# A running sum of router masks moves from GpSimd to the vector engine, and positions are worked out in float

## The chip, the cores and the metric

The kernel runs on one core of a Trainium2 chip, as one launch. A core has five engines with an instruction stream each: the tensor engine (PE, matmuls and transposes), the vector engine (DVE), the scalar engine (ACT), GpSimd (POOL) and SyncE (SP), which here issues most DMAs. Each engine runs its instructions in the order in which they were written; between engines, and between two instructions of one engine where one reads what the other wrote, the program waits on semaphores. The metric is device time in microseconds of one execution, lower is better.

## The reference, cut to what matters

Two layers of gated cross-attention with a feed-forward block run on 4 x 1024 tokens of 256 features. The first layer's feed-forward block is a mixture of 64 experts, 8 per token, with at most 128 tokens for each expert. What the change touches is the place of each token in its expert's list:

```python
w, idx = jax.lax.top_k(probs, TOP_K)
e_flat = idx.reshape(-1)
tok = jnp.arange(A) // TOP_K
onehot = jax.nn.one_hot(e_flat, E, dtype=jnp.int32)
pos = jnp.take_along_axis(jnp.cumsum(onehot, axis=0) - 1, e_flat[:, None], axis=1)[:, 0]
slot = jnp.minimum(pos, CAPACITY)
buf = jnp.zeros((E, CAPACITY + 1, H), x.dtype).at[e_flat, slot].set(x[tok])
```

The position of a token is the number of earlier tokens that picked the same expert.

## The kernel before

The kernel has three stages: the first layer's attention with the router, the experts (with the shared expert and the preparation of the second layer's weights beside them), and the second layer. Only the first stage, up to some 345 us, holds lines that the change touches.

The first stage goes over eight halves of 512 tokens (`h` from 0 to 7; each batch of 1024 tokens has two). A half has four tiles of 128 tokens. Its main work is the attention over 154 keys for 16 heads: PE computes scores (L838 to L841) into five banks of PSUM, ACT makes two passes over them (`square` L1200, `root` L1205), DVE one (`weight`, L1557, 0.68 us a time), and PE multiplies the weights with the values (L862, L867). Beside it run, each in small steps, the keys of the next batch (`key_mask`, L1512 and L1514, before every second half), the queries of the next half (PE L827, DVE `q_high` L1545 and `q_low` L1551 into `q_stage`), the end of the attention of the half before (transposes L884, `divide` L1563 and L1565, output projection L908 and L913, `x_add` L1578), and the router.

The router of a half: `gate` gives 64 logits per token; DVE takes the eight highest (`top`, L1604), marks them (`pick`: L1611 and then L1616, which writes `masks`, four tiles of 128x64, ones and zeros); PE's `count` multiplies the masks with a triangular matrix and with ones, and adds the product of ones with `mask_sums` (called `before` in the code), the number of picks per expert and lane in all halves before this one. `mask_sums` has two places that take turns; for the next half the new one is the old one plus the four tiles of masks. In the kernel before, POOL makes these four adds (`count` of the GpSimd program, L2009). DVE's `position` (L1636) takes the product of `count` out of PSUM, subtracts 4096 where a token picked the expert, and writes integers; `ranks` (L1641, L1643, L1646, L1647) splits them into the part over 16 and the rest, both as bf16 in `pos_a` and `pos_b`, which lie in the tile `w_con_fused`. From these, `hots` (L1745, L1748) makes one-hot tiles later, from which PE builds the lists of tokens (L1026).

The order is fixed when the program is built. A planner lays the units of all streams into slots, with tables that say in which slot of the attention each step of a half goes; every engine then runs the units that it has a part in, in the order of the one plan. `pick`, `count`, `position` and `ranks` stand in it one after another for each half, with attention units, and in places keys and queries, between them. PE's part of `count` and DVE's `position` share a bank of PSUM with the queries, keys and projections (two banks, `misc`, in turn).

Of the kernel before, what the change touches and what calls it, by code (L numbers as in the profile page):

```python
# [14 lines left out]
ALU = mybir.AluOpType  # L15
# [14 lines left out]
HT = HALF // P  # L30
HALVES = TOKENS // HALF
# [27 lines left out]
NB = 16  # L59
# [3 lines left out]
FAR = 4096.0  # L63
# [434 lines left out]
def build(nc, D, out):  # L498
    ctx = ExitStack()
    with ctx:  # L500
# [13 lines left out]
        misc = Ring(bank[6:8], sems("misc_full", 2), sems("misc_free", 2))  # L514
# [19 lines left out]
        rstd = [sb(f"rstd{i}", [P, HT], F32) for i in range(2)]  # L534
# [17 lines left out]
        with ExitStack() as scope:  # L552
# [35 lines left out]
            masks = s0("masks", [P, HT, EXPERTS], BF16)  # L588
# [187 lines left out]
        def tensor_program(T):  # L776
# [155 lines left out]
            def count(h):  # L932
                key = ("count", h)
                if h == 0:
                    T.wait_ge(upper_in, 16)
                    T.wait_ge(pool_set, POOL_FIRST)
                else:
                    T.wait_ge(summed, HT * h)
                T.wait_ge(masked, h + 1)
                T.wait_ge(*misc.vacant(key))  # L940
                for t in range(HT):
                    here = misc.ap(key)[:, t * EXPERTS:(t + 1) * EXPERTS]
                    T.matmul(here, upper[:, :], masks[:, t, :], start=True, stop=False)
                    for u in range(t):
                        T.matmul(here, ones[:, :], masks[:, u, :], start=False, stop=False)
                    m = T.matmul(here, ones[:, :], before[:, h % 2, :], start=False, stop=True)
                m.then_inc(misc.fills(key), 1)
# [467 lines left out]
        def vector_program(V):  # L1415
            own = Own()
# [190 lines left out]
            def pick(h):  # L1607
                first = gated_tiles(h).start
                V.wait_ge(dve_own, own.n)
                for t in range(HT):  # L1610
                    m = V.match_replace(picked[:, t, :], top[:, first + t, :], probs[:, first + t, :], 1.0)  # L1611
                m.then_inc(dve_own, own.up())
                if h:
                    V.wait_ge(summed, HT * h)
                V.wait_ge(dve_own, own.n)
                V.tensor_scalar(masks[:, :, :], picked[:, :, :], 0.0, None, ALU.is_gt).then_inc(masked, 1)  # L1616

            def gate_weights(b):
# [10 lines left out]
                                       gate_sums[:, 0, :].unsqueeze(2).to_broadcast([P, GATED_TILES, EXPERTS]),  # L1629
                                       ALU.mult, ALU.mult).then_inc(rows_set, 1)  # L1630

            def position(h):
                key = ("count", h)
                counts = misc.ap(key)[:, 0:HT * EXPERTS].rearrange("p (t n) -> p t n", n=EXPERTS)
                V.wait_ge(*misc.filled(key))
                V.scalar_tensor_tensor(pos_i[:, 0, :, :], masks[:, :, :], -FAR, counts, ALU.mult,  # L1636
                                       ALU.add).then_inc(misc.frees(key), 1)

            def ranks(h):
                V.wait_ge(*misc.freed(("count", h)))  # L1640
                V.tensor_scalar(pos_i[:, 1, :, :], pos_i[:, 0, :, :], 4, None,  # L1641
                                ALU.arith_shift_right).then_inc(dve_own, own.up())
                V.tensor_scalar(pos_i[:, 0, :, :], pos_i[:, 0, :, :], NB - 1, None,  # L1643
                                ALU.bitwise_and).then_inc(dve_own, own.up())
                V.wait_ge(dve_own, own.n)
                V.tensor_scalar(pos_a[:, HT * h:HT * h + HT, :], pos_i[:, 1, :, :], FAR / NB, None, ALU.add)  # L1646
                V.tensor_copy(pos_b[:, HT * h:HT * h + HT, :], pos_i[:, 0, :, :])  # L1647


# [225 lines left out]
            def out_add(h, b, k):  # L1875
                if k == BURST - 1:
# [4 lines left out]
                    for two in range(HT // 2):  # L1881
# [7 lines left out]
            units = {"bn": bn, "highest": highest_, "ranks": ranks, "q_high": q_high, "q_low": q_low, "stats": stats_, "norm": norm, "key_mask": key_mask, "bias_parts": set_bias_parts, "key_rest": key_rest,  # L1889
                     "set_values": set_values, "weight": weight,  # L1890
                     "divide": divide, "x_add": x_add, "shift": shift, "top": top_, "pick": pick,
                     "gate_weights": gate_weights, "position": position, "sh_split": sh_split_, "sh_up": sh_up,
                     "sh_inner": sh_inner_, "sh_down": sh_down, "taps": set_coef, "matrix": stage_matrix, "across": across,
                     "hid_bias": set_hid_bias, "out_bias": set_out_bias, "hots": hots, "lists": set_lists,
                     "tokens": set_tokens, "gate_up": gate_up, "down": down, "add_experts": add_experts,
# [12 lines left out]
        def gpsimd_program(G):  # L1908
# [86 lines left out]
                    G.tensor_tensor(w_sd[:, 1], sd_staged, w_sd[:, 0].bitcast(F32),  # L1995
                                    ALU.subtract).then_inc(sh_split, 1)

            def count(h):
                if h == HALVES - 1:
                    return  # L2000
                old, new = before[:, h % 2, :], before[:, (h + 1) % 2, :]
                G.wait_ge(masked, h + 1)
                if h:
                    G.wait_ge(*misc.filled(("count", h - 1)))
                    G.wait_ge(summed, HT * h)
                for t in range(HT):
                    if t:
                        G.wait_ge(summed, HT * h + t)
                    G.tensor_tensor(new, new if t else old, masks[:, t, :], ALU.add).then_inc(summed, 1)  # L2009

            def set_query_ones(i):
                G.wait_ge(pool_set, set_.n)
                G.memset(q_stack[i][STACK:ROWS0, :, :].bitcast(F32), 1.0).then_inc(pool_set, set_.up())
# [8 lines left out]
            def clear_rest():  # L2022
# [14 lines left out]
            G.memset(k_masked[:, :, 2, :], 0.0).then_inc(pool_set, set_.up())  # L2037
            set_query_ones(0)
            G.wait_ge(pool_set, set_.n)
            units = {"count": count, "sh_weights": sh_weights, "sh_split": sh_split_, "rstd": norm_rstd, "load_rest": clear_rest, "gather": gather, "down": scatter,  # L2040
                     "add_experts": add_experts, "bias_out": bias_out, "up": hidden_rest, "clear_v1": clear_v1}
            for n, plan in enumerate((first, experts, last)):
                if n == 2:
# [350 lines left out]
```

## Time and profile before

| What | Value |
| --- | --- |
| Median of 3 runs | 1139.92 us (1139.42 to 1140.05) |
| The profiled execution | 1139.42 us |
| Its span, first to last instruction | 1137.6 us |
| Mean granted clock of PE | 0.957 of full speed |
| Busy: PE, DVE, ACT, POOL | 989.6, 777.7, 622.1, 402.9 us |
| Chain that ended last, by engine | PE 54%, DVE 22%, ACT 9%, POOL 4%, DMA 3% |
| First stage, 0 to 344 us: PE, DVE, ACT, POOL busy | 292.9, 281.0, 245.9, 56.9 us |

Instructions of one engine overlap a little at their ends, so the start of one can lie before the end of the one ahead. The chain of waits is followed back from the last instruction to what released it, or to the instruction ahead of it on its engine; a piece in it is the time from one such step to the next. A window's row gives the busy time of each engine, with the number of instructions in brackets.

### The profile page before, as it was taken

What the parts mean: (1) busy time and instruction counts of PE and PEld (TensorE: products, weight loads), DVE (VectorE), ACT (ScalarE), POOL (GpSimd) and SP (SyncE); (2) the same over time, 40 slices, a digit from 0 to 9 for tenths busy, and PEclk for the clock granted to TensorE, in tenths of its full rate; (3) what the DMA queues carried; (4) which work ended last, traced back from release to release, by engine and by line L of the source; (5) the groups of instructions that cost most, each with busy time, mean ns of one, the idle gap of its engine ahead of it and who ended that gap; (6) DMA issues with size and microseconds to landing.
All of it is one profiled execution on the core that took longest, in us unless ns stands there. A gap on an engine that the chain in (4) does not pass through costs nothing.

```text
span 1137.6 us, 16837 instructions
## 1 busy us (share of the span) xinstructions
PE 989.6 (87%) x5379; PEld 702.5 (62%) x5379; DVE 777.7 (68%) x1951; ACT 622.1 (55%) x1204; POOL 402.9 (35%) x417
## 2 busy tenths in 40 slices
PE   4899999999769699998999758788898989989988
PEld 2355555555447488776887636466667666757657
DVE  4688989987787566657675666866775676664443
ACT  1887888879465245546554213654554555454532
POOL 6000111102020257677776222152525252504234
PEclk9899999999979899999999958899999999999999
DMA  6737466453114378888876533413231412110000
GB/s 139 205 73 214 141 175 171 109 151 112 56 52 152 107 175 192 195 231 209 211 178 133 131 85 100 100 35 113 58 94 28 113 51 86 29 49 1 21 19 19
DMA packets 101559, 128.38 MB, mean 113 GB/s; under 512 B 31136, under 2 KB 73504, under 8 KB 101216
## 3 DMA queue, kind: packets, MB, share of 16 engines
q1 hardware_dynamic: 87088, 106.32, 32.8%
q0 software_dynamic: 12288, 18.88, 9.3%
q10 hardware_dynamic: 2096, 2.10, 0.8%
q8 instruction: 44, 0.72, 0.3%
q14 instruction: 43, 0.35, 0.1%
HBM read 66.15 MB, written 30.70 MB: 85 GB/s over the span
## 4 chain that ended last, share of the span: by engine, by line
PE 54%; DVE 22%; ACT 9%; issue 5%; POOL 4%; DMA 3%; SPq 1%; ACTq 1%; DVEq 0%; POOLq 0%
PE psum L960 6%; PE psum L1144 6%; PE psum L1129 5%; PE psum L1049 4%; PE psum L976 4%; PE psum L867 3%; PE psum L838 3%; DVE peaks L1825 3%; DVE stats L1421 2%; PE psum L913 2%; PE psum L784 2%; PE psum L827 2%; PE psum L1076 2%; PE psum L862 2%; DVE weights L1557 2%
## 5 line engine op out<-in xcount | busy, mean ns | idle before, releaser
L1924 POOL TENSOR_SCALAR vareps<-moments 128x4 f32<-128x4 f32 x32 | 12.2, 382 | 350.0 <-DVE moments L1431 350.0
L838 PE MATMUL psum<-q_stack,k_stack 97*128 97x512 f32 (+1 forms) x256 | 118.3, 488 | 20.2 <-DVE weights L1557 7.2
L1355 ACT ACTIVATE weights<-psum 128x512 f32<-128x512 f32 x160 | 92.9, 595 | 65.6 <-PE psum L838 57.5
L1947 POOL DMA_INDIRECT expert_sums<-made,sum_rows x64 | 104.1, 1626 | 63.6 <-DVE made L1789 44.4
L1076 PE MATMUL psum<-k_stack,q_stack 96*128 96x308 f32 x256 | 86.3, 399 | 36.5 <-DVE peaks L1825 24.6
L1557 DVE SCALAR_TENSOR_TENSOR weights<-weights,psum 128x512 f32<-128x512 f32 x160 | 102.7, 681 | 17.8 <-ACT weights L1205 17.5
L1825 DVE TENSOR_REDUCE peaks<-psum 128x2 f32<-128x308 f32 x256 | 105.8, 470 | 7.7 <-PE psum L1076 7.5
L1979 POOL TENSOR_TENSOR hidden<-hidden_whole,hidden 128x512 fp32r<-128x512 f32 x64 | 82.9, 1300 | 60.7 <-DVE hidden L1873 60.7
L960 PE MATMUL psum<-feat_parts,w_shared_up 128*128 128x512 f32 x384 | 98.4, 406 | 4.2 <-DVE shared_silu L1663 2.6
L1076 PEld LDWEIGHTS psum<-k_stack,q_stack 96*128 96x128 f32 x256 | 50.8, 203 | 81.7 <-DVE peaks L1825 40.1
L1144 PE MATMUL psum<-w_con_high,hidden 128*128 128x256 f32 x512 | 100.7, 295 | 0.5 <-POOL hidden L1979 0.5
L1200 ACT ACTIVATE weights<-psum 128x512 f32<-128x512 f32 x160 | 89.1, 596 | 20.7 <-PE psum L838 20.0
L1873 DVE CAST hidden<-hidden_whole 128x512 fp32r<-128x512 f32 x64 | 45.9, 725 | 77.5 <-ACT hidden_whole L1384 77.0
L1939 POOL DMA_INDIRECT got<-rows_scratch,tokens x64 | 68.3, 1068 | 76.5 <-issue 73.7
L1205 ACT ACTIVATE weights<-weights 128x512 f32<-128x512 f32 x160 | 94.0, 633 | 1.0
L1129 PE MATMUL psum<-feats,w_up_high 128*128 128x512 f32 x256 | 80.4, 411 | 11.3 <-ACT hidden_whole L1384 6.4
L1144 PEld LDWEIGHTS psum<-w_con_high,hidden 128*128 128x128 f32 x512 | 81.2, 190 | 13.3 <-POOL hidden L1979 7.6
L960 PEld LDWEIGHTS psum<-feat_parts,w_shared_up 128*128 128x128 f32 x384 | 71.4, 193 | 19.9 <-DVE shared_silu L1663 3.3
L838 PEld LDWEIGHTS psum<-q_stack,k_stack 97*128 97x128 f32 (+1 forms) x256 | 48.0, 192 | 56.2 <-issue 19.8
L1384 ACT ACTIVATE hidden_whole<-psum,hidden_bias 128x512 f32<-128x512 f32 x64 | 42.6, 687 | 66.2 <-PE psum L1129 48.0
L1049 PEld LDWEIGHTS psum<-got_t,expert_w 128*128 128x128 f32 x512 | 64.3, 191 | 23.0 <-ACT got_t L1311 14.5
L1049 PE MATMUL psum<-got_t,expert_w 128*128 128x128 f32 x512 | 70.3, 280 | 8.9 <-DVE inner L1782 4.1
(210 smaller groups left out, 2219.9 us busy)
## 6 DMA issues: line engine op xcount, KB each, us to landing
expert_w<-in_expert_w SPq DMA_DIRECT2D x64, 384.0 KB
q_stack<-q_stage SPq DMA_DIRECT2D x96, 128.0 KB, 2.4
q_stack<-q_stage SPq DMA_DIRECT2D x174, 64.0 KB, 2.0
expert_sums<-zeros SPq DMA_DIRECT2D x6, 1408.0 KB, 8.6
fetched<-expert_sums SPq DMA_DIRECT2D x14, 512.0 KB, 4.5
k_raw<-in_k SPq DMA_DIRECT2D x16, 300.0 KB
x<-in_x SPq DMA_DIRECT2D x8, 512.0 KB, 4.8
rows_scratch<-rows SPq DMA_DIRECT2D x8, 512.0 KB, 3.5
```

The lines of the kernel that those rows point to most:

```text
L838: T.matmul(to, keys_of(h, head), q[0:row, head // 2, :], start=True, stop=True).then_inc(scored, 1)
L960: m = T.matmul(shared_banks(h).ap(key, half), w_sgu[:, pw, a:a + P], sh_parts[:, pf, c * HALF:(c + 1) * HALF], start=n == 0 and c == 0, st ...
L1049: m = T.matmul(bank[2][:, part * P:(part + 1) * P], expert_w[e % 8][:, c, part * INNER:(part + 1) * INNER], got_t[e % 3][:, c, :], start=c ...
L1076: T.matmul(wide.ap(key, i)[:, 0:2 * KEYS], q[0:STACK, p, t * P:(t + 1) * P], keys[0:STACK, 2 * KEYS * p:2 * KEYS * (p + 1)], start=True, s ...
L1129: m = T.matmul(wide.ap(key), up_parts[pw][:, c, k * P:(k + 1) * P], feats[:, pf, c, :], start=i == 0 and c == 0, stop=i == 2 and c == CD - 1)
L1144: m = T.matmul(out_bank[t // 2][:, t % 2 * DIM:(t % 2 + 1) * DIM], hidden[k][:, ph, t * P:(t + 1) * P], con_parts[pw][:, BURST * b + k, :] ...
L1200: A.activation(weights[n % 9][:, :], score_bank[n % 5], ACT.Square, bias=2.0, scale=-1.0).then_inc(squared, 1)
L1205: A.activation(weights[n % 9][:, :], weights[n % 9][:, :], ACT.Abs_reciprocal_sqrt).then_inc(exped, 1)
L1355: A.activation(weights1[n % 6][:, :], score_bank[n % 2], ACT.Exp).then_inc(exped, 1)
L1557: V.scalar_tensor_tensor(weights[n % 9][:, :], weights[n % 9][:, :], 1.0, score_bank[n % 5], ALU.min, ALU.max).then_inc(weighted, 1)
L1825: V.tensor_reduce(peaks[:, t, 2 * p:2 * p + 2], view, AX.X, ALU.max).then_inc(wide.frees(key, i), 1)
L1947: G.indirect_dma_start(sum_dram[e % SUMS], bass.IndirectOffsetOnAxis(ap=sum_rows[:, e:e + 1], axis=0), made[e % 4][:, :], None, bounds_che ...
```

## The change

The four adds of `count` move from POOL to DVE. There each add waits for the one ahead, and the semaphore `summed` rises once for a half, no longer once for an add; what waits for it waits for `h` instead of `4 * h`. The wait in `pick` for `summed` is dropped. `position` is three instructions now: the product goes to the float tile `picked`, 4096 is added there, and a copy casts to integers, which are now the positions themselves where a token picked the expert, and values from 4096 up where it didn't. In `ranks` the shift becomes a logical one, a wait is put between it and the mask of the low bits, and a plain copy takes the place of an add of 256.

```diff
@@ PE, count
-                    T.wait_ge(summed, HT * h)
+                    T.wait_ge(summed, h)
@@ DVE, pick
-                if h:
-                    V.wait_ge(summed, HT * h)
                 V.wait_ge(dve_own, own.n)
@@ DVE
+            def count(h):
+                if h == HALVES - 1:
+                    return
+                old, new = before[:, h % 2, :], before[:, (h + 1) % 2, :]
+                V.wait_ge(masked, h + 1)
+                for t in range(HT):
+                    if t:
+                        V.wait_ge(dve_own, own.n)
+                    elif h:
+                        V.wait_ge(summed, h)
+                    m = V.tensor_tensor(new, new if t else old, masks[:, t, :], ALU.add)
+                    if t < HT - 1:
+                        m.then_inc(dve_own, own.up())
+                m.then_inc(summed, 1)
+
             def position(h):
...
-                V.scalar_tensor_tensor(pos_i[:, 0, :, :], masks[:, :, :], -FAR, counts, ALU.mult,
+                V.scalar_tensor_tensor(picked[:, :, :], masks[:, :, :], -FAR, counts, ALU.mult,
                                        ALU.add).then_inc(misc.frees(key), 1)
+                V.wait_ge(*misc.freed(key))
+                V.tensor_scalar(picked[:, :, :], picked[:, :, :], FAR, None, ALU.add).then_inc(dve_own, own.up())
+                V.wait_ge(dve_own, own.n)
+                V.tensor_copy(pos_i[:, 0, :, :], picked[:, :, :]).then_inc(dve_own, own.up())
 
             def ranks(h):
-                V.wait_ge(*misc.freed(("count", h)))
+                V.wait_ge(dve_own, own.n)
                 V.tensor_scalar(pos_i[:, 1, :, :], pos_i[:, 0, :, :], 4, None,
-                                ALU.arith_shift_right).then_inc(dve_own, own.up())
+                                ALU.logical_shift_right).then_inc(dve_own, own.up())
+                V.wait_ge(dve_own, own.n)
                 V.tensor_scalar(pos_i[:, 0, :, :], pos_i[:, 0, :, :], NB - 1, None,
                                 ALU.bitwise_and).then_inc(dve_own, own.up())
                 V.wait_ge(dve_own, own.n)
-                V.tensor_scalar(pos_a[:, HT * h:HT * h + HT, :], pos_i[:, 1, :, :], FAR / NB, None, ALU.add)
+                V.tensor_copy(pos_a[:, HT * h:HT * h + HT, :], pos_i[:, 1, :, :])
@@ POOL
-            def count(h):
...
-                for t in range(HT):
-                    if t:
-                        G.wait_ge(summed, HT * h + t)
-                    G.tensor_tensor(new, new if t else old, masks[:, t, :], ALU.add).then_inc(summed, 1)
```

The first place is DVE's row in halves 1 and 3, from the masks to the first query step and the position, before the change (`k_masked` is the key masking, `weights` the attention's weights):

```order
L1616 TENSOR_SCALAR masks<-picked 128x256
L1512 TENSOR_SCALAR k_masked<-psum,bk,side_of 128x128 x2
L1514 SCALAR_TENSOR_TENSOR k_masked<-psum,bk,place_of 128x4x26
L1512 TENSOR_SCALAR k_masked<-psum,bk,side_of 128x128 x2
L1514 SCALAR_TENSOR_TENSOR k_masked<-psum,bk,place_of 128x4x26
L1545 TENSOR_SCALAR q_stage<-psum,bq 128x512
L1551 SCALAR_TENSOR_TENSOR q_stage<-psum,bq,q_stage 128x512
L1557 SCALAR_TENSOR_TENSOR weights<-weights,psum 128x512 x2
L1636 SCALAR_TENSOR_TENSOR pos_i<-masks,psum 128x256
```

And the same place after it:

```order
L1514 SCALAR_TENSOR_TENSOR k_masked<-psum,bk,place_of 128x4x26
L1640 TENSOR_TENSOR mask_sums<-mask_sums,masks 128x64 x4
L1545 TENSOR_SCALAR q_stage<-psum,bq 128x512
L1551 SCALAR_TENSOR_TENSOR q_stage<-psum,bq,q_stage 128x512
L1557 SCALAR_TENSOR_TENSOR weights<-weights,psum 128x512 x2
L1649 SCALAR_TENSOR_TENSOR picked<-masks,psum 128x256
L1652 TENSOR_SCALAR picked<-picked 128x256
L1654 CAST pos_i<-picked 128x256
```

The four adds stand between the key masking and the query step, and two more instructions behind the product. In halves 0, 2 and 4 there is no key masking, and the adds follow the masks at once. The second place is DVE in half 6, where the attention is nearly over; `sums` and `att` are the division of a tile's attention. Before:

```order
L1616 TENSOR_SCALAR masks<-picked 128x256
L1636 SCALAR_TENSOR_TENSOR pos_i<-masks,psum 128x256
L1563 RECIPROCAL sums<-psum 128x16
L1565 TENSOR_TENSOR att<-psum,sums 128x256
L1641 TENSOR_SCALAR pos_i<-pos_i 128x256
L1643 TENSOR_SCALAR pos_i<-pos_i 128x256
```

After:

```order
L1614 TENSOR_SCALAR masks<-picked 128x256
L1640 TENSOR_TENSOR mask_sums<-mask_sums,masks 128x64 x4
L1649 SCALAR_TENSOR_TENSOR picked<-masks,psum 128x256
L1652 TENSOR_SCALAR picked<-picked 128x256
L1654 CAST pos_i<-picked 128x256
L1563 RECIPROCAL sums<-psum 128x16
L1565 TENSOR_TENSOR att<-psum,sums 128x256
L1658 TENSOR_SCALAR pos_i<-pos_i 128x256
L1661 TENSOR_SCALAR pos_i<-pos_i 128x256
```

Six instructions more stand between the masks and the division here. In half 7 no adds are made, since no half follows. The rows of PE and ACT are the same before and after; POOL loses its 28 adds and keeps the order of the rest.

## Rows read from the trace of the kernel before

**Rows 1.** Windows view: PE, PEld, DVE, ACT, POOL busy (instructions); clock, DMA share, GB/s.
```profile
80.00:240.00 160.00, 150.92 (x790) 85.74 (x786) 145.92 (x409) 129.75 (x244) 20.64 (x40) 1.00 0.59 162
```

**Rows 2.** Waits, 60 to 340 us: us in total, times, longest us.
```profile
POOL mask_sums L2009 <- DVE masks L1616: 53.4, 7, 10.9
PEld psum L943 <- POOL mask_sums L2009: 0.9, 2, 0.5
```

**Rows 3.** Line 2009: duration ns min/median/max, first and last start, form.
```profile
L2009 POOL TENSOR_TENSOR mask_sums<-mask_sums,masks x28: 304/306/309, 96.9 to 295.0; 128x64 bf16<-128x64 bf16 x28
```

**Rows 4.** Groups on DVE, 60 to 340 us: busy us, mean ns, idle before.
```profile
L1748 DVE TENSOR_TENSOR hot_b<-b_iota,w_con_fused 128x1024 bf16<-128x1024 bf16 x21 | 14.4, 685 | 0.0
L1745 DVE TENSOR_TENSOR hot_a<-a_iota,w_con_fused 128x512 bf16<-128x512 bf16 x22 | 9.2, 420 | 2.2 <-PE psum L1026 2.2
L1474 DVE TENSOR_SCALAR normed<-x,moments,rstd 128x256 f32<-128x256 f32 x20 | 6.9, 413 | 0.0
L1588 DVE COPY sgate<-psum 128x4 f32<-128x4 f32 x8 | 1.2, 154 | 0.0
```

**Rows 5.** Timeline of DVE, ranks of half 7: start us, us, instruction.
```profile
335.24 0.29 DVE L1641 TENSOR_SCALAR pos_i<-pos_i 128x256 int32<-128x256 int32 x1
335.44 0.29 DVE L1643 TENSOR_SCALAR pos_i<-pos_i 128x256 int32<-128x256 int32 x1
335.77 0.29 DVE L1646 TENSOR_SCALAR w_con_fused<-pos_i 128x256 bf16<-128x256 int32 x1
```

**Rows 6.** Timeline of DVE, halves 0, 2 and 4: start us, us, instruction, idle before.
```profile
97.76 0.75 DVE L1545 TENSOR_SCALAR q_stage<-psum,bq 128x512 fp32r<-128x512 f32 x1 [0.94 <-PE psum L827]
...
101.37 0.75 DVE L1545 TENSOR_SCALAR q_stage<-psum,bq 128x512 fp32r<-128x512 f32 x1 [0.56 <-PE psum L827]
...
113.20 0.75 DVE L1578 SCALAR_TENSOR_TENSOR x<-psum,tanh_gates,x 128x512 f32<-128x512 f32 x1 [0.33 <-PE psum L913]
...
165.20 0.75 DVE L1545 TENSOR_SCALAR q_stage<-psum,bq 128x512 fp32r<-128x512 f32 x1 [0.86 <-PE psum L827]
...
234.38 0.75 DVE L1545 TENSOR_SCALAR q_stage<-psum,bq 128x512 fp32r<-128x512 f32 x1 [0.79 <-PE psum L827]
```

**Rows 7.** Chain of waits, half 1: start us, us, piece.
```profile
130.89 0.10 DVE k_masked L1514
131.04 0.76 DVE q_stage L1545
132.63 2.00 PE psum L827 x4
```

**Rows 8.** Chain of waits, ranks of half 3.
```profile
212.00 0.20 DVE pos_i L1641
```

**Rows 9.** Timeline of DVE, half 5.
```profile
265.40 0.29 DVE L1616 TENSOR_SCALAR masks<-picked 128x256 bf16<-128x256 f32 x1
...
265.61 1.28 DVE L1557 SCALAR_TENSOR_TENSOR weights<-weights,psum 128x512 f32<-128x512 f32 x2
...
267.74 0.25 DVE L1563 RECIPROCAL sums<-psum 128x16 f32<-128x16 f32 x1
...
269.20 0.26 DVE L1563 RECIPROCAL sums<-psum 128x16 f32<-128x16 f32 x1 [0.76 <-PE psum L884]
```

**Rows 10.** Timeline of DVE, half 6.
```profile
293.52 0.29 DVE L1616 TENSOR_SCALAR masks<-picked 128x256 bf16<-128x256 f32 x1
294.52 0.42 DVE L1636 SCALAR_TENSOR_TENSOR pos_i<-masks,psum 128x256 int32<-128x256 bf16 x1 [0.71 <-PE psum L946]
295.06 0.26 DVE L1563 RECIPROCAL sums<-psum 128x16 f32<-128x16 f32 x1
```

**Rows 11.** Chain of waits, position of half 7.
```profile
334.06 0.33 DVE pos_i L1636
```

**Rows 12.** Timeline of DVE, rows of half 7.
```profile
315.33 5.00 DVE L1474 TENSOR_SCALAR rows<-x,moments,rstd 128x256 f32<-128x256 f32 x3 [1.64 <-POOL rstd L1929]
```

**Rows 13.** Timeline of POOL beside it.
```profile
315.17 2.34 POOL L1992 TENSOR_TENSOR feat_parts<-feats_m,feat_parts 128x1024 fp32r<-128x1024 f32 x1
```

More of the change, by code:

```diff
@@ L1891, in vector_program @@
                      "divide": divide, "x_add": x_add, "shift": shift, "top": top_, "pick": pick,
-                     "gate_weights": gate_weights, "position": position, "sh_split": sh_split_, "sh_up": sh_up,
+                     "gate_weights": gate_weights, "count": count, "position": position, "sh_split": sh_split_, "sh_up": sh_up,
                      "sh_inner": sh_inner_, "sh_down": sh_down, "taps": set_coef, "matrix": stage_matrix, "across": across,
@@ L1996, in sh_split_ @@
                                     ALU.subtract).then_inc(sh_split, 1)
-            def count(h):
[L1999 to L2005, printed above, removed]
-                for t in range(HT):
-                    if t:
-                        G.wait_ge(summed, HT * h + t)
-                    G.tensor_tensor(new, new if t else old, masks[:, t, :], ALU.add).then_inc(summed, 1)
             def set_query_ones(i):
@@ L2039, in gpsimd_program @@
             G.wait_ge(pool_set, set_.n)
-            units = {"count": count, "sh_weights": sh_weights, "sh_split": sh_split_, "rstd": norm_rstd, "load_rest": clear_rest, "gather": gather, "down": scatter,
+            units = {"sh_weights": sh_weights, "sh_split": sh_split_, "rstd": norm_rstd, "load_rest": clear_rest, "gather": gather, "down": scatter,
                      "add_experts": add_experts, "bias_out": bias_out, "up": hidden_rest, "clear_v1": clear_v1}
```

## The prediction

> **What bounds the kernel now.** I read the busy time by windows first, then the chain of waits, then the waits of the moved work, then the timeline of the vector engine (DVE) around each of the eight halves (0 to 7) of 512 tokens. The change touches only the first stage. There the tensor engine (PE) is busy 150.9 of 160 us and DVE 145.9, at a granted clock of 1.00, while GpSimd (POOL) is busy 20.6 [rows 1]. PE and DVE take turns: the reader is to see in the chain that DVE pieces stand on it wherever PE waits for a result (a DVE `q_stage`, then PE's query projection, [rows 7]), and that DVE has only short gaps of its own. So a DVE instruction costs its full time where no gap follows, and nothing where one does. The working goes by place, not by the sum of busy time.
>
> **What is removed.** POOL loses 28 adds of 0.306 us, 8.6 us [rows 3]. POOL sat 53.4 us waiting for the masks before them; the only wait charged to them is 0.9 us in 2 cases, on PE's load for the count [rows 2]. That product reads the running sum of the half before, finished a half earlier, so the charge is to a releaser long done. I take the removal at 0, with 0.9 us as the most it could give. The wait on `summed` in `pick` goes too; it was for the half before, so nothing is late in its place. PE's count still waits for the masks alone in effect.
>
> **Unit prices on DVE.** The profile shows two spacings of a 256-column instruction of 0.29 us. Without a wait in between the next starts 0.20 after (335.24 to 335.44); where it waits for the one ahead, 0.33 after (335.44 to 335.77) [rows 5]. So a waited instruction costs its duration + 0.04, an unwaited one its duration - 0.09.
> - Add 128x64 bf16: not shown. 1024 columns take 0.685 and 512 take 0.420 [rows 4]; the line through both gives 0.265 per 512 and 0.155 fixed, so 64 columns take 0.155 + 0.033 = 0.19. Bounds: 0.154, the smallest copy [rows 4], and 0.306, POOL's own time [rows 3]. I take 0.19, since its two rows are the same kind of operation and type.
> - Scale-and-add and cast of 128x256 f32 in SBUF: not shown in these types. The nearest are the 0.29 us ones on int32 [rows 5]; bounds 0.154 and 0.413, a 128x256 f32 operation with two scalars per partition [rows 4]. I take 0.29, by the like form.
> - The product of masks and counts keeps its 0.42 us [rows 10]; only its output goes to a float tile.
>
> So `count` is four adds, each waiting for the one ahead: in a dense run 3 x 0.23 + 0.10 = 0.79 us; right behind the masks it waits for them too, 0.04 + 3 x 0.23 + 0.10 = 0.83 after their end. `position` becomes three instructions: product 0.42 + 0.04, scale-and-add 0.33, cast 0.20 = 0.99 to the next one, where 0.33 was needed [rows 11]: +0.66 in a dense run, or 0.57 after the product's end. `ranks` gets one more wait between its first two: 0.33 - 0.20 = +0.13.
>
> The trace shows 0.13 us between the waited and the unwaited start [rows 5]. The Trainium skill (VectorE: DVE Perf Modes, section The DRAIN you can't avoid) says the opposite, that a semaphore between operations of DVE costs nothing extra, since the next has to wait for the pipeline to empty anyway. By that rule the added waits would be free; this trace disagrees, and the case stands below as a rival worked from the unwaited spacing.
>
> **The sum, half by half.**
> - Halves 0, 2, 4: `count` lands in the gap ahead of `q_stage`, where DVE waited 0.94, 0.86 and 0.79 us for PE's projection [rows 6]. It needs 0.83: 0, 0 and +0.04.
> - `position` in halves 0 to 4 lands in a gap too, 0.56 us ahead of the second `q_stage` of half 0 [rows 6], with four more of the same kind. It needs 0.57: +0.01 each, 0.05.
> - Half 1: between the masks and `q_stage` stands the key masking. The chain runs from its last piece at 130.89 into `q_stage` at 131.04, then PE's projection at 132.63 [rows 7]; no gap. `count` goes in exactly there: +0.79. Behind `q_stage` are queued its low part, PE's second projection and all the weights that follow.
> - Half 3: the same layout, +0.79; and here the chain passes through `ranks` too (212.00, [rows 8]): +0.13. In halves 0, 1, 2 and 4 a gap for PE's output projection follows `ranks` (0.33 at 113.20, [rows 6]) and takes the 0.13. Together 0.92.
> - Half 5: no keys, no queries; weights follow the masks at once (265.40, 265.61). `count` moves them by 0.83 + 0.29 - 0.21 = 0.91, `position` adds 0.66: 1.57. The gap ahead of the reciprocal at 269.20 was 0.76 [rows 9]: DVE was free at 268.44, now at 270.01, and the reciprocal starts 0.09 before that, 269.92. PE's weighing moves by less. +0.72.
> - Half 6: masks 293.52, the adds fill the 0.71 gap and overrun it: product at 293.52 + 0.29 + 0.83 = 294.64 rather than 294.52, reciprocal at 294.64 + 0.99 = 295.63 rather than 295.06 [rows 10], +0.57; `ranks` right behind, +0.13. 0.70.
> - Half 7: no count. The chain is DVE alone there, the product with 0.33 [rows 11] and then one-hots: 0.66 + 0.13 = 0.79.
>
> Sum: 0.04 + 0.05 + 0.79 + 0.92 + 0.72 + 0.70 + 0.79 = 4.0 us. What follows (the tail of the stage, the experts, the second layer) has no work changed and starts that much later. The profiled execution took 1139.42 us (its span 1137.6 and 1.8 around it), so 1143.4; against the median of the three runs, 1139.92, which lies 0.5 above it, 1143.9 us.
>
> Both ends: adds at 0.154 take 0.04 off each of four in halves 1, 3, 5 and 6 and the 0.04 of half 4, -0.7; the two new f32 operations at 0.154 take another 0.27 per half in 5, 6 and 7, -0.8: +2.5. Adds at 0.306 add 0.46 per half in 1, 3, 4, 5, 6 and 0.35 and 0.43 in 0 and 2, +3.1; the f32 operations at 0.413 add 0.24 in all eight, +1.9: +9.0.
>
> **Rivals.**
> 1. Waits inside DVE cost nothing. Adds are then 0.10 apart, `count` 0.40, `position` +0.40, `ranks` 0. Halves 1 and 3 give 0.40 each, 7 gives 0.40, 6 gives 0.19 (its product stays at 294.52, the reciprocal goes to 295.25), 5 next to nothing: +1.4, 1141.3 us. Against it stand the 0.20 and 0.33 of [rows 5]. 5%. The rule of the Trainium skill quoted above would have it so.
> 2. The new instructions are long, near the upper bounds, by a slower mode of the f32 ones or a longer small add: +6 to +9, about 1147 us. For it: the 0.413 row has the same shape and type [rows 4]. Against: 0.29 for all three forms of [rows 5]. 12%.
> 3. The clock falls once more, because PE idles a little longer. It stood at 1.00 in the attention [rows 1]; one projection of 2.00 us [rows 7] at the lower level (1.2 instead of 2.4 GHz) would take 4.00: +2 on top, 1145.9 us. 8%.
> 4. Not slower: the stage's tail gives it back. At 315.33 three `rows` instructions of DVE take 5.00 us [rows 12] where such a shape takes 0.413 each [rows 4], beside POOL's split from 315.17 [rows 13]. If `rows` got clear of the split, some 3.7 us would come back: +0.3, 1140.2 us. It decides on whether the split starts 1.1 us or more later against `rows` than it does (three instructions of 0.413 being done by then). Against: both stand behind POOL's `rstd`, and both move with DVE's one-hots. 5%.
> 5. Halves 1 and 3 don't bind: another path through PE, with slack of a microsecond, takes their 0.79 and 0.92, and the 0.9 of [rows 2] was real: +1.4, 1141.3 us. Against: the chain runs through both places without a gap [rows 7, 8]. 5%. Only rivals 4 and 5 together, 1137.6, or something unseen, would come out faster.
>
> **How the numbers follow.** The forecast has 65%, between 1142.4 and 1146; the rivals 5, 12, 8, 5 and 5. About 0.2% (2.3 us) is what a measurement of this kernel can tell from no change, so same is 1137.6 to 1142.2. Rivals 1, 4 and 5 lie there, 15%, less the 3% that I give to faster: same 0.12; faster by more than that 0.03; slower 0.85. The range goes from just above rivals 1 and 5, at 1141.5, up through rival 3 and the nearer part of rival 2 to 1147.3.
>
> **What would show it.** The four adds on DVE at 0.19 each, 0.23 apart; the two f32 instructions at 0.29; DVE's busy time in the first stage up by some 10 us (28 x 0.19 + 16 x 0.29) and POOL's down by 8.6. `q_stage` of halves 0, 2 and 4 still waiting for PE with next to no gap, that of halves 1 and 3 late by 0.8 and PE's projection behind it too. Against a same-numbered event of before the lag should be 0.8 after half 1, 1.8 after half 3, 2.6 after half 5, 3.3 after half 6, and 4.0 when the experts start, and stay. I would be wrong if PE's projection in half 1 is not late, if the adds start 0.10 apart, or if the lag shrinks in the tail at the `rows` instructions.

## The result, and the profile after

The changed kernel is slower: 1145.4 us in the median of 6 runs (1144.32 to 1147.23) against 1139.31 (1136.51 to 1140.05) for the kernel before, measured beside it, a ratio of 1.0059 with a 95% interval of 1.0046 to 1.0072. Measured a second time, with the last experiments, it was 1.0049 (1.0034 to 1.0065). The forecast was 1143.9 us, +4.0, where +6.1 came; the time lies inside the range of 1141.5 to 1147.3. The profiled execution took 1145.61 us, its span is 1143.8 us, 6.2 more than before.

The windows view of the changed kernel, 80 to 240 us, with the columns of [rows 1]:

```profile
80.00:240.00 160.00, 148.59 (x776) 84.83 (x773) 150.19 (x436) 127.75 (x240) 14.47 (x20) 1.00 0.59 162
```

DVE is busy for 150.2 of 160 us now, 4.3 more, and POOL for 14.5, 6.2 less; PE does less in the same stretch of time, since its work runs later. Over the whole span DVE's busy time went from 777.7 to 788.8 us.

The new instructions, by line (duration in ns: least, median, most; first and last start; form):

```profile
L1640 DVE TENSOR_TENSOR mask_sums<-mask_sums,masks x28: 181/192/193, 96.7 to 297.3; 128x64 bf16<-128x64 bf16 x28
```

```profile
L1652 DVE TENSOR_SCALAR picked<-picked x8: 293/294/295, 101.0 to 337.7; 128x256 f32<-128x256 f32 x8
```

```profile
L1654 DVE CAST pos_i<-picked x8: 293/294/295, 101.3 to 338.0; 128x256 int32<-128x256 f32 x8
```

So the adds take 0.192 us where 0.19 was estimated, and the two float instructions 0.294 where 0.29 was.

To see where the time went, take the same event in both traces and subtract the starts: the lag is how much later the event comes in the changed kernel. The two executions differ by 0.18 us before the first changed instruction; that is taken off. Lag in us, worked out from the timelines of DVE:

| Event | Lag | Forecast by then |
| --- | --- | --- |
| `q_stage` of half 0, behind the adds | 0.35 | 0 |
| `q_stage` of half 1 | 1.26 | 0.8 |
| `q_stage` of half 3 | 2.15 | 1.6 |
| `x_add` of half 3, behind `ranks` | 2.29 | 1.75 |
| `q_stage` of half 4 | 2.36 | 1.8 |
| reciprocal of half 5 (269.20 before) | 3.05 | 2.6 |
| one-hot behind `ranks` of half 6 | 3.65 | 3.3 |
| one-hot behind `ranks` of half 7 | 4.23 | 4.0 |
| last shared-expert step ahead of the lists | 4.40 | 4.0 |
| expert 7's `inner`, some 50 us on | 6.05 | 4.0 |

The last row holds the part that the forecast had not: 1.7 us appear behind the lists, where no instruction was changed.

The timeline of DVE after, in halves 0, 1 and 4 (start us, us, instruction; the idle time before it and what ended it in brackets), beside [rows 6, 7]:

```profile
96.67 0.87 DVE L1640 TENSOR_TENSOR mask_sums<-mask_sums,masks 128x64 bf16<-128x64 bf16 x4
97.93 0.75 DVE L1545 TENSOR_SCALAR q_stage<-psum,bq 128x512 fp32r<-128x512 f32 x1 [0.38 <-issue]
...
131.24 0.86 DVE L1640 TENSOR_TENSOR mask_sums<-mask_sums,masks 128x64 bf16<-128x64 bf16 x4
132.12 0.75 DVE L1545 TENSOR_SCALAR q_stage<-psum,bq 128x512 fp32r<-128x512 f32 x1
...
235.67 0.87 DVE L1640 TENSOR_TENSOR mask_sums<-mask_sums,masks 128x64 bf16<-128x64 bf16 x4
236.56 0.75 DVE L1545 TENSOR_SCALAR q_stage<-psum,bq 128x512 fp32r<-128x512 f32 x1
```

In half 4 the adds fill the gap that DVE had and overrun it by little. In half 1 `q_stage` starts 0.88 after the first add (0.79 was forecast). In half 0 the adds end at 97.54, PE's projection at 97.44, and still `q_stage` starts only at 97.93. The reader is to see that "issue" stands where PE stood in [rows 6]: DVE waits for nothing that the profile shows.

The clock's part. Windows view behind the lists, before:

```profile
375.00:380.00 5.00, 3.74 (x17) 3.77 (x18) 1.01 (x6) 0.00 (x0) 2.31 (x2) 0.50 0.95 339
380.00:385.00 5.00, 3.92 (x15) 2.88 (x13) 3.26 (x18) 1.18 (x3) 4.00 (x4) 0.81 0.57 186
385.00:390.00 5.00, 3.06 (x11) 1.51 (x11) 4.67 (x15) 3.14 (x8) 0.00 (x0) 1.00 0.13 38
```

And after, 4 us later, the same work:

```profile
379.00:384.00 5.00, 3.55 (x17) 3.48 (x17) 1.16 (x6) 0.00 (x0) 2.27 (x2) 0.50 0.95 328
384.00:389.00 5.00, 5.00 (x16) 3.93 (x15) 2.31 (x16) 1.17 (x3) 3.78 (x5) 0.55 0.60 197
389.00:394.00 5.00, 2.78 (x8) 1.47 (x7) 4.33 (x13) 1.62 (x5) 0.25 (x1) 0.79 0.16 51
```

The column behind POOL's is the granted clock of PE: 0.50 is the lower level, 1.2 GHz, 1.00 the upper, 2.4 GHz. PE had stood idle for the lists in both. Afterwards before's second window is at 0.81 and the third back at 1.00; after's are at 0.55 and 0.79. The chain shows the price on one group of matmuls, before and after:

```profile
380.44 3.49 PE psum L960 x12
```

```profile
384.73 4.56 PE psum L960 x12
```

The same twelve matmuls of the shared expert took 1.07 us longer. The next group of matmuls on the chain, before and after:

```profile
387.88 0.71 PE psum L1008 x2
```

```profile
392.20 2.28 PE psum L1008 x4
```

By the lag of the instructions of DVE around them, the first group took the lag from 4.48 to 5.54 and the second to 6.06: all that appears behind the lists.

The lag does not stay at 6.0 after that. It is 7.6 us at 900 us of the kernel before and 6.3 at its end. These steps in the second layer were not followed up.

### The profile page after: what moved, and what is told of

Read it like the earlier page. It is cut to its first block, busy times and chain, and to the rows that moved or that the text cites. A ratio compares the mean times of both kernels' runs of the same rounds, so it can differ in the third digit from the quotient of the medians.

```text
span 1143.8 us, 16846 instructions
## 1 busy us (share of the span) xinstructions
PE 992.2 (87%) x5379; PEld 703.9 (62%) x5379; DVE 788.8 (69%) x1995; ACT 621.7 (54%) x1204; POOL 393.6 (34%) x389
## 4 chain that ended last, share of the span: by engine, by line
PE 53%; DVE 25%; ACT 9%; issue 6%; POOL 3%; DMA 2%; SPq 1%; ACTq 1%; DVEq 0%; POOLq 0%
PE psum L960 6%; PE psum L1144 5%; PE psum L1129 5%; PE psum L1049 4%; PE psum L976 4%; PE psum L838 3%; PE psum L867 3%; DVE weights L1557 3%; DVE peaks L1843 3%; DVE stats L1421 2%; PE psum L913 2%; PE psum L784 2%; PE psum L1008 2%; PE psum L1076 2%; PE psum L862 2%
## 5 line engine op out<-in xcount | busy, mean ns | idle before, releaser
L960 PE MATMUL psum<-feat_parts,w_shared_up 128*128 128x512 f32 x384 | 99.5, 409 | 4.9 <-DVE shared_silu L1681 2.6
L960 PEld LDWEIGHTS psum<-feat_parts,w_shared_up 128*128 128x128 f32 x384 | 72.1, 194 | 21.2 <-DVE shared_silu L1681 3.5
```

The source lines that it names most:

```text
L960: m = T.matmul(shared_banks(h).ap(key, half), w_sgu[:, pw, a:a + P], sh_parts[:, pf, c * HALF:(c + 1) * HALF], start=n == 0 and c == 0, st ...
```

## The experiments

All are compared with the kernel before on the same chip. Where a lag is given, it is worked out from the profiles like the table above. Single executions of the kernel before ranged from 1135.7 to 1144.6 us in 23 runs beside the last experiments, so the lags tell more of a single place than the ratios. A lag at expert 7 is not the lag at the end, as the changed kernel shows.

### Only the adds moved

```diff
 # the changed kernel, with position and ranks as before
-                V.scalar_tensor_tensor(picked[:, :, :], masks[:, :, :], -FAR, counts, ALU.mult,
+                V.scalar_tensor_tensor(pos_i[:, 0, :, :], masks[:, :, :], -FAR, counts, ALU.mult,
                                        ALU.add).then_inc(misc.frees(key), 1)
```

> The changed kernel with position and ranks as they were before: only the four adds are on DVE. Theory A (place by place: an add costs only where no gap of DVE follows): +0.4 in half 0, +0.8 in half 1, +0.8 in half 3, under 0.1 in half 4, +0.1 in half 5 (0.91 against a gap of 0.76), 0 in half 6, so the one-hots of half 7 are 2.1 us late; the end 2.1 to 4 us late, by how much PE's work behind the lists falls on the lower clock. Rival B (by busy time): 28 adds of 0.23 = 6.4 us late in the first stage.

Ratio 1.0025 (1.0005 to 1.0045), about 2.9 us by the ratio. Lag: 0.35 in half 0, 0.89 in half 1, 0.87 in half 3, 0.17 in half 4, 0.70 in half 5, none in half 6: 2.9 us at the one-hots of half 6, not 2.1. Theory B with its 6.4 falls. Theory A holds but for half 5, where 0.70 came and 0.1 was expected. The chain of waits of this kernel in half 5 says why:

```profile
268.58 0.19 DVE mask_sums L1640
268.77 0.61 DVE weights L1557
269.38 0.14 issue
269.52 0.47 PE psum L838
269.99 0.03 issue
270.02 0.49 PE psum L838
270.52 0.99 PE psum L867 x8
```

The weights behind the adds are what PE's next scores wait for (a bank of PSUM comes free with them), then its weighing, then the transposes that the reciprocal waits for. The gap of 0.76 at the reciprocal [rows 9] was behind that loop and could take nothing of it.

Behind half 6, where this kernel has no changed instruction left, its lag goes on from 2.9 to 4.2 us ahead of half 7 and is 4.9 at expert 7. Between 305 and 310 us the granted clock is 0.68 here and 1.00 in the kernel before. So the lags of the two halves of the change, taken apart, do not add up to that of the whole: 4.9 and 3.4 at expert 7 against 6.0.

### Only the positions in float

```diff
 # the kernel before, with the new position and ranks; count stays on POOL
-                V.scalar_tensor_tensor(pos_i[:, 0, :, :], masks[:, :, :], -FAR, counts, ALU.mult,
+                V.scalar_tensor_tensor(picked[:, :, :], masks[:, :, :], -FAR, counts, ALU.mult,
```

> The kernel before with the new position and ranks, the adds on POOL. Theory A: nothing in halves 0 to 2 and 4, +0.13 in half 3, 0 in half 5 (0.66 within its gap of 0.76), +0.6 in half 6, +0.8 in half 7: 1.5 us late at the end of the first stage, less than the whole minus the adds, since half 5's gap is used by either part alone. Rival B: 8 x 0.79 = 6.3 us. The end is 1.5 to 3.5 us late.

Ratio 1.0019 (1.0005 to 1.0033), about 2.2 us. Lag 0.04 up to half 3, 0.18 behind its `ranks`, no more in half 5, 0.73 after half 6; in half 7 it grew by 0.78 between the one-hot ahead of `position` and the one behind `ranks`. That is 1.5 us as theory A had it; between half 6 and half 7 another 1.9 came at one blow, where this kernel's clock was at the lower level for longer. In half 6 every price of the forecast can be read off, the timeline of this kernel:

```profile
293.88 0.42 DVE L1636 SCALAR_TENSOR_TENSOR picked<-masks,psum 128x256 f32<-128x256 bf16 x1 [0.71 <-PE psum L946]
294.33 0.29 DVE L1639 TENSOR_SCALAR picked<-picked 128x256 f32<-128x256 f32 x1
294.67 0.29 DVE L1641 CAST pos_i<-picked 128x256 int32<-128x256 f32 x1
294.87 0.25 DVE L1563 RECIPROCAL sums<-psum 128x16 f32<-128x16 f32 x1
```

Starts 0.45, 0.34 and 0.20 apart: 0.99, as forecast.

### Spare adds, with and without waits

```diff
 # the kernel before, POOL's adds kept; on DVE, behind pick
+                V.wait_ge(masked, h + 1)
+                for t in range(HT):
+                    if t:
+                        V.wait_ge(dve_own, own.n)      # left out in the second kernel
+                    m = V.tensor_tensor(apart[:, t, :], masks[:, t, :], masks[:, t, :], ALU.add)
```

With the waits:

> The kernel before, POOL's adds kept, and four adds of the same size on DVE at the place of the change, each waiting for the one ahead, into a tile that nothing reads. Theory A (POOL's adds cost nobody anything): the same as with only the adds moved, 2.1 us late at the end of the first stage, within 0.1. Rival C (taking the adds from POOL was worth something, up to the 0.9 us charged to them): later than that kernel by up to 0.9 us in the first stage.

Without them:

> The same spare adds without the waits between them. Theory A (a waited instruction costs its duration + 0.04, an unwaited one its duration - 0.09): the four adds start 0.10 apart, 0.40 in a dense run, so 0.8 us late at the end of the first stage (halves 1 and 3) against 2.1 with the waits. Rival D (the wait costs nothing, as the Trainium skill has it, VectorE: DVE Perf Modes, section The DRAIN you can't avoid): the adds start as far apart as with the waits, 0.23, and the lag is the same 2.1.

Timeline of the kernel with waits, half 1:

```profile
132.21 0.86 DVE L1639 TENSOR_TENSOR below_tables<-masks 128x64 bf16<-128x64 bf16 x4
133.09 0.75 DVE L1545 TENSOR_SCALAR q_stage<-psum,bq 128x512 fp32r<-128x512 f32 x1
```

Of the one without:

```profile
131.86 0.49 DVE L1637 TENSOR_TENSOR below_tables<-masks 128x64 bf16<-128x64 bf16 x4
132.26 0.75 DVE L1545 TENSOR_SCALAR q_stage<-psum,bq 128x512 fp32r<-128x512 f32 x1
```

The same four adds on the same operands need 0.88 us to the next instruction with the waits and 0.40 without. Rival D, that the wait costs nothing, is out for these short instructions; 0.40 is what the forecast's spacing gives. In the lag at the one-hots of half 6 it is 3.8 against 1.7 us; the ratios are 1.0038 (1.0022 to 1.0053) and 1.0022 (1.0009 to 1.0036), in the same order, with intervals that overlap.

Rival C seemed to get its 0.9: this kernel is 3.8 us late where the one that moved the adds is 2.9. But the cause is another. In halves 0, 2, 4, 5 and 6 one of the four adds or two take longer, as in half 5:

```profile
269.27 1.02 DVE L1639 TENSOR_TENSOR below_tables<-masks 128x64 bf16<-128x64 bf16 x4
```

Here POOL makes its adds of the same tiles at the same time; the most that one add of DVE took is 0.341, against 0.193 where POOL had none. One of POOL's adds took 0.36 for 0.31. It happens in the halves where the adds follow the masks at once, not in 1 and 3, where the key masking lies between (0.86 above). Each of those five halves brings 0.14 to 0.24 us more lag than in the kernel that only moved the adds, which makes up the 0.9; in halves 5 and 6 some 0.08 of it is the wait that `pick` keeps here. So the two sets of adds disturb each other when they run together; that POOL's alone had cost anybody something isn't shown.

### The waits for the query stacks ahead of the adds

```diff
             def count(h):
...
+                if h < 5:
+                    wait_all(V, q_in[h % 2], h // 2 + 2)
                 V.wait_ge(masked, h + 1)
...
             def q_high(h, mo):
-                if h and mo == 0:
+                if 0 < h < 3 and mo == 0:
                     wait_all(V, q_in[(h - 1) % 2], (h - 1) // 2 + 1)
```

> The changed kernel with the four waits of q_high for the query stacks (DMAs landed long ago) put ahead of the adds, so that DVE's queue works them off before the masks are ready or in the adds' shadow. Theory E (in half 0 the first q_stage started 0.41 us after PE's projection had ended because the queue had five waits to work off behind the last add): the 0.41 goes to 0.05 in half 0, and halves 1, 3 and 4 gain about 0.1 each; the lag of the first stage falls from 4.3 to about 3.7 us. Rival F (the 0.41 has another cause, such as the add's own end): unchanged at 4.3.

The lag in half 0 went from 0.35 to 0, in halves 1 and 3 from 0.89 and 0.88 to 0.78 and 0.77, which is the forecast's 0.79; half 4 rose by 0.1, and the one-hots of half 6 are 3.16 us late, not 3.65. `wait_all` is four waits in DVE's queue for transfers long landed. Standing behind the adds, they delayed `q_stage` by 0.1 in halves 1 and 3; standing ahead of them, they didn't.

In half 0 the lag goes when the waits are moved, but theory E's reason for it, waits to be worked off behind the last add, does not hold. The kernel with the spare adds unwaited has the same 0.35 there, though its adds were over before PE was done. Its DVE and its PE:

```profile
97.32 0.61 DVE L1637 TENSOR_TENSOR below_tables<-masks 128x64 bf16<-128x64 bf16 x4
98.57 0.75 DVE L1545 TENSOR_SCALAR q_stage<-psum,bq 128x512 fp32r<-128x512 f32 x1 [0.64 <-PE psum L827]
```

```profile
96.09 1.98 PE L827 MATMUL psum<-q_feats,wq 128*128 128x512 f32 x4 [0.33 <-ACT q_feats L1169]
```

The adds end at 97.93, PE at 98.07, and `q_stage` starts at 98.57, 0.50 later; in the kernel before it starts 0.14 after PE's end. What holds it up in half 0 is open. The ratio, 1.0051 (1.0027 to 1.0075), can't tell half a microsecond.

### A pure delay of three sizes

```diff
 # the kernel before, behind ranks of half 7; 7, 13 or 20 copies
+                if h == HALVES - 1:
+                    for _ in range(7):
+                        V.wait_ge(dve_own, own.n)
+                        V.tensor_copy(picked[:, :, :], probs[:, 0:HT, :]).then_inc(dve_own, own.up())
```

> The kernel before with 7 spare copies on DVE, each waiting for the one ahead (0.33 us), right behind ranks of half 7, where the chain is DVE alone: a pure delay of 2.3 us at the end of the first stage. Theory G (the 1.8 us beyond the 4.3 come from PE's work behind the lists falling on more of a stretch at the lower clock, by where the delay puts it): the end is late by 2.3 plus an amount that is not proportional to it, 0 to 2 us, with the granted clock of that stretch to show it. Rival H (each microsecond of delay costs 1.4, by something that the later stages have in proportion): 3.2 us late.

> The same with 13 spare copies, a pure delay of 4.3 us, the size of the change's. Theory G: what the change showed, some 6 us late at the end, of which 1.8 behind the lists on the lower clock. Rival I (the 1.8 come from something in the change itself): 4.3 us late. Rival H: 6.0.

> The same with 20 spare copies, 6.6 us. Theory G: 6.6 plus 0 to 2, not in line with the two smaller ones. Rival H: 9.2 us late.

| Copies | Put in (profile) | Lag ahead of the lists | Lag at expert 7 | Ratio |
| --- | --- | --- | --- | --- |
| 7 | 2.2 | 2.9 | 3.3 | 1.0025 (1.0012 to 1.0039) |
| 13 | 4.1 | 6.3 | 6.5 | 1.0044 (1.0027 to 1.0061) |
| 20 | 6.4 | 9.4 | 9.7 | 1.0079 (1.0060 to 1.0098) |

The second kernel has the delay of the change and nothing else of it, and it too is 6.5 us late at expert 7: a lag beyond what was put in needs no changed instruction, which is against rival I. The places differ: with 13 copies 2.1 us come in the shared expert ahead of the lists, where this kernel's clock fell in a stretch in which before's was at 1.00, between 355 and 365 us:

```profile
355.00:360.00 5.00, 3.92 (x22) 3.31 (x23) 3.60 (x7) 2.83 (x5) 0.00 (x0) 0.77 0.12 47
360.00:365.00 5.00, 5.00 (x40) 4.92 (x40) 3.88 (x10) 2.43 (x4) 0.00 (x0) 0.88 0.29 105
```

With 7 copies the lag goes up by 0.7 and back, and then by 0.7 and 0.4, in different places. Between theory G (by where the clock falls) and rival H (1.4 for 1) the times can't decide: rival H's 3.2, 6.0 and 9.2 us lie in all three intervals (1.4 to 4.4, 3.1 to 6.9, 6.8 to 11.2). Nor do these three profiles decide it by size: the lag at expert 7 is 1.5, 1.6 and 1.5 times what was put in, near rival H's 1.4. That it rises in steps and is flat between them is for G.

The profiles of the other kernels decide it. Lag in us ahead of the lists and at expert 7, and the two groups of matmuls on the chain behind the lists:

| Kernel | Ahead of the lists | At expert 7 | L960, x12 | L1008 |
| --- | --- | --- | --- | --- |
| Before | 0 | 0 | 3.49 | 0.71 |
| Changed | 4.4 | 6.0 | 4.56 | 2.28 |
| Changed, again | 4.4 | 6.2 | 4.69 | 2.28 |
| Adds in a gap (below) | 1.5 | 2.9 | 4.37 | 2.27 |
| 7 copies | 2.9 | 3.3 | 3.90 | 0.71 |
| Only the adds moved | 4.8 | 4.9 | 3.44 | 0.71 |
| Spare adds with waits | 4.0 | 3.9 | 3.44 | 0.71 |
| Waits ahead of the adds | 4.0 | 3.7 | 3.34 | 0.71 |

The chain of the last of these:

```profile
384.66 3.34 PE psum L960 x12
391.95 0.71 PE psum L1008 x2
```

It has all instructions of the change, comes to the lists 4.0 us late, and nothing is added behind them, while the kernel with the adds in a gap comes 1.5 us late and 1.4 are added. So the part behind the lists is neither in the changed instructions (rival I) nor in proportion to the delay (rival H). It is in the matmuls each time: with 7 copies the twelve take 0.41 longer and 0.4 is added. Between 390 and 395 us the granted clock is 0.69, 0.78 and 0.79 in the three kernels to which 1.4 us or more is added, and 1.00 in the other five.

### The adds in a gap

```diff
 # the changed kernel; the planner puts the adds of halves 0 to 5 one slot ahead of ranks
         put(route_steps(h), first, R_AT)
+        if h < 6:
+            slots.setdefault(first + 49, []).append(("adds", h))
```

> The changed kernel with the adds of halves 0 to 5 put one slot ahead of ranks, where DVE waits 0.87 us for ACT's weights in every half; half 6 keeps them where they are. Theory A (an add costs by its place): no lag up to half 5 but 0.13 for the wait in ranks of half 3, less about 0.08 a half that the wait for the running sum in pick no longer takes; then half 6 about 0.6 and half 7 0.75: 1.5 us late at the one-hots of half 7, 3 us earlier than the changed kernel, with the same instructions. Rival J (it is DVE's total work that costs): 4.4 us late as the changed kernel.

Timeline of this kernel, half 3:

```profile
209.75 0.68 DVE L1559 SCALAR_TENSOR_TENSOR weights<-weights,psum 128x512 f32<-128x512 f32 x1
210.35 0.86 DVE L1642 TENSOR_TENSOR mask_sums<-mask_sums,masks 128x64 bf16<-128x64 bf16 x4
211.31 0.69 DVE L1559 SCALAR_TENSOR_TENSOR weights<-weights,psum 128x512 f32<-128x512 f32 x1
...
212.23 0.29 DVE L1663 TENSOR_SCALAR pos_i<-pos_i 128x256 int32<-128x256 int32 x1
```

In the kernel before, the gap was there:

```profile
211.32 0.69 DVE L1557 SCALAR_TENSOR_TENSOR weights<-weights,psum 128x512 f32<-128x512 f32 x1 [0.87 <-ACT weights L1205]
```

The adds lie whole between two weights of which the second waits for ACT anyway. Lag: at most 0.06 up to half 3, 0.15 behind its `ranks` (the new wait), 0.10 in half 5, 0.72 after half 6, and 1.06 at the one-hots of half 7, since 0.4 was won back in between. The same instructions as in the changed kernel, 2.9 us less of lag after half 6. Rival J is out. Ratio 1.0029 (1.0016 to 1.0042), 3.1 us under the changed kernel in the medians (1141.74 against 1144.88, same chip).

### The changed kernel again

> The changed kernel again, unaltered, beside the two below. All theories: first stage 4.4 us late again; the end 4.4 us late plus what the clock does, 5 to 7 us (ratio 1.004 to 1.006).

1144.88 us, 1.0049 (1.0034 to 1.0065). Its lags repeat the first profile's within 0.12: 0.35, 1.22, 2.10, 2.97 (half 5), 3.59 (half 6), 4.31 (half 7), then 6.17 at expert 7.

### The kernel before, its ranks in the gap

```diff
 # the kernel before; ranks of halves 0 to 5 at first + 49, and
             def pick(h):
-                if h:
-                    V.wait_ge(summed, HT * h)
...
             def ranks(h):
+                if h < HALVES - 1:
+                    V.wait_ge(summed, HT * (h + 1))
```

> The kernel before with ranks of halves 0 to 5 moved into that same gap, and pick's wait for the running sum moved along with it. Theory A: half 3, where the chain runs through ranks, gains up to 0.9 us, the wait 0.08 in each of halves 5 to 7: 1 to 1.2 us earlier than the kernel before (ratio 0.999), which these rounds can hardly tell, but the profile can, event by event. Rival: the weights behind the gap come later by what ranks overruns it (0.94 against 0.87), and nothing is gained.

Up to half 6 it did as theory A says: 0.94 us early from half 3 on, 1.08 after half 6. And there the gain was lost. Windows view of this kernel, 300 to 310 us, where the kernel before had 0.66 and 1.00:

```profile
300.00:305.00 5.00, 4.32 (x14) 3.01 (x15) 3.48 (x8) 3.17 (x6) 0.00 (x0) 0.50 0.01 3
305.00:310.00 5.00, 5.00 (x22) 3.69 (x21) 1.68 (x3) 0.72 (x1) 0.00 (x0) 0.82 0.00 0
```

Its chain has the output projection at

```profile
303.58 3.53 PE psum L915 x8
```

against 1.92 us for the same eight matmuls in the kernel before. Further on it has sixteen matmuls at

```profile
324.65 3.31 PE psum L930 x16
```

against 1.87. By half 7 it is 2.7 us late, 3.8 lost, of which these two groups make up some 3. Ratio 1.0011 (0.9998 to 1.0025): no version here is shown to beat the kernel before.

## Why the prediction was right, and what was off

- **What bounds the kernel.** Right: the adds cost by place. The kernel with the adds in a gap shows it most plainly; the sum of DVE's busy time (11 us more) tells nothing of the 4.2 us of lag in the stage.
- **The removal at 0.** Nothing contradicts it. The waits of 0.9 us in 2 cases that were charged to POOL's adds stand under "issue" now (7.6 us in 6 cases before, 8.3 in 8 after), so nothing is seen to be won by their going. One small thing was missed: the wait on `summed` that `pick` lost. The wait is met long before, but `masks` started 0.32 us after the last L1611 in half 1 before (128.45 to 128.77) and 0.24 after it now (128.64 to 128.88). So it had cost 0.08, and taking it away is the -0.06 of half 5 in the kernel with the adds in a gap.
- **Unit prices.** Right to 0.01 us, from a line through two larger sizes and from two starts in [rows 5]. The waited and unwaited spacings of 0.23 and 0.10 held, and rival 1, by which a wait between two instructions of DVE is free, did not.
- **Half 0, forecast 0.01, measured 0.37.** Wrong: the sum took `q_stage` as ready when the adds and PE were done. It started 0.39 us after the later of the two. The cause is open: the delay comes with adds that end before PE does as well as with those that end after it, and goes when four waits are moved ahead of the adds.
- **Halves 1 and 3, forecast 0.80 and 0.93, measured 0.91 and 1.01.** The mechanism was right, the term 0.1 too small in each, by the four waits ahead of `q_stage`: moved, they gave the 0.1 back.
- **Half 5, forecast 0.72, measured 0.69.** Right for a wrong reason. The forecast added `count` and `position` and took one gap off. The two halves of the change apart show that the adds cost 0.70 by themselves and the positions nothing: the adds sit in the loop of weights and scores, the positions in the gap behind it.
- **Halves 6 and 7, forecast 0.70 and 0.79, measured 0.60 and 0.71.** Right; 0.08 each was the wait that `pick` lost. Between the two halves another 0.12 us of lag went away, where nothing was changed.
- **The sum.** The terms of the first stage came to 4.2 us of lag where 4.0 was forecast, but partly by luck: 0.36 too little in half 0 and 0.2 in halves 1 and 3 stand against 0.2 too much in halves 6 and 7 and the 0.12 between them. The checkpoints 2.6 and 3.3 of the prediction are 2.5 and 3.2 by its own terms.
- **The step that failed: "has no work changed and starts that much later", and the lag that was to stay.** The lag was 4.4 us ahead of the lists and 6.0 and 6.2 at the experts, in two profiles. The instructions there are the same, and one group of twelve took 4.56 us for 3.49 at a lower granted clock. The forecast had the clock as rival 3, at +2 for one projection, near what came, but in the attention, and with 8%; from 80 to 240 us the clock stayed at 1.00. It belonged in the sum's own uncertainty, at the places where PE stands idle. The time of 1145.4 us still lies in the band of 1142.4 to 1146 that the forecast gave 65%, but near its top, with a third of the 6.1 us in a term that the sum had at nothing.
- **Rival 4**, the tail that gives it back, did not come: `rows` and POOL's split moved together, as the forecast argued. The four `rows` take 5.32 us in both kernels.

Shown are the prices, the places and the cost of the waits but for half 0. That the extra 1.7 us are the clock's rests on the clock column and the longer matmuls: both are there in the three profiles that have 1.4 us or more of it, and both are missing in three kernels that come as late to the lists, 4.0 to 4.8 us, and have none. The clock itself can't be held still, so no run takes it away alone, and each kernel but the changed one was profiled once. What decides where it falls was not tried.

## What to carry to other kernels

Look for the gap before you move an instruction to the busiest engine: the same four adds cost nothing in front of a wait for another engine and their whole length in a dense run, and the slot can be chosen. A gap is worth only what lies behind it: one that closes a loop through another engine does not absorb what is put inside the loop. And a small delay, or a small gain, can come out at nearly twice its size (1.5 us became 2.9) or with the other sign (1.1 early became 2.7 late) where the granted clock changes after PE was idle; judge changes of a microsecond by the lag of single events, not by the total.

## What the runs showed of the hardware that was not expected

- A wait that is long met still takes time on DVE's queue when no gap hides it: 0.08 us for the one in `pick`, 0.1 for the four ahead of `q_stage`.
- Four adds of 128x64 on DVE that each wait for the one ahead take 0.78 to 0.88 us up to the next instruction, without these waits 0.40: half of the time is the waiting for one's own engine.
- Adds on DVE and on POOL over the same tiles at the same time lengthen one of DVE's from 0.193 to as much as 0.341 us and one of POOL's from 0.306 to 0.363.
- Being 1.08 us early turned into 2.7 us late within one stretch of the kernel, in its one profile: eight matmuls took 3.53 us for 1.92 and sixteen 3.31 for 1.87, where the granted clock was lower.
